# Rows of attention projected before they are weighed, the last rows added in halves, and filler products left out

## The reference

```python
x = x + tanh(g_xattn[0]) * attention(norm(x), ctx, wq, wk, wv, wo)   # keys and values: context rows, then own rows
x = x + tanh(g_ffn[0])   * swiglu_ternary(norm(x), w1, w3, w2)       # weights rounded to -1, 0, 1 times their mean size
x = x + tanh(g_xattn[1]) * wkv(decay, bonus, norm(x), ctx)           # a recurrence over the 64 rows of a sequence
x = x + tanh(g_ffn[1])   * experts(norm(x), router, shared, experts) # 2 of 8 experts for each row, and a shared one
```

```python
out  = softmax(q @ concat(ctx, k).T / 16) @ concat(ctx, v)
return out @ wo.T
```

## Time and profile before

| | |
|---|---|
| time, median of 3 runs | 769.02 us (768.88 to 769.07) |
| the profiled execution | 771.49 us |
| its span, first to last instruction | 769.6 us |
| TensorE busy | 725.0 us, 94% |
| VectorE, ScalarE, GpSimd busy | 520.2, 352.4, 330.5 us |
| mean granted clock of TensorE | 0.99 of full speed |

### The profile page before, as it was taken

One profiled execution on the slowest core, in us unless ns is written; L12 is line 12 of the kernel. 1 busy time (PEld: TensorE's weight loads), 2 busy tenths in 40 slices (PEclk: granted clock), 3 DMA queues, 4 the chain that ended last, 5 costly groups with the idle time before them and its releaser, 6 DMA issues. The chain is left out here.

```text
span 769.6 us, 13097 instructions
## 1 busy us (share of the span) xinstructions
PE 725.0 (94%) x4624; PEld 621.1 (81%) x4624; DVE 520.2 (68%) x926; ACT 352.4 (46%) x676; POOL 330.5 (43%) x345
## 2 busy tenths in 40 slices
PE   6998998999999999999999999999999999897996
PEld 6886787788878988788877988788877988686785
DVE  2778586747877387756877478746877477698532
ACT  3556525642465435643465435553365434523231
POOL 2004204543537155443538155453537245275354
PEclk8999999999999999999999999999999999999999
DMA  9142020200122003111032002110022010011111
GB/s 266 52 138 82 1 56 1 68 30 28 49 76 58 28 29 83 55 41 27 21 85 72 27 27 82 55 41 27 14 82 83 19 35 27 29 42 41 56 63 47
DMA packets 36211, 41.24 MB, mean 54 GB/s; under 512 B 3198, under 2 KB 27476, under 8 KB 36180
## 3 DMA queue, kind: packets, MB, share of 16 engines
q1 hardware_dynamic: 36180, 40.83, 17.8%
HBM read 36.49 MB, written 4.33 MB: 53 GB/s over the span
## 5 line engine op out<-in xcount | busy, mean ns | idle before, releaser
L1136 POOL TENSOR_TENSOR hid_l<-act_sb,hid_h 128x512 fp32r<-128x512 f32 x120 | 163.3, 1361 | 205.9 <-ACT hid_h L938 205.6
L1384 DVE SCALAR_TENSOR_TENSOR act_sb<-act_sb,gate_ps 128x512 f32<-128x512 f32 (+1 forms) x128 | 86.7, 678 | 113.0 <-ACT act_sb L920 112.9
L1145 POOL TENSOR_TENSOR act_sb<-act_sb,late 128x512 f32<-128x512 f32 x64 | 93.6, 1462 | 74.1 <-DVE act_sb L1386 71.5
L938 ACT ACTIVATE hid_h<-act_sb 128x512 fp32r<-128x512 f32 (+1 forms) x128 | 80.3, 627 | 95.6 <-POOL act_sb L1145 62.6
L482 PE MATMUL sums<-down_h,hid_h 128*128 128x256 f32 x320 | 92.0, 288 | 5.0 <-POOL hid_l L1136 5.0
L482 PE MATMUL sums<-down_h,hid_l 128*128 128x256 f32 x320 | 90.3, 282 | 0.0
L482 PE MATMUL sums<-down_l,hid_h 128*128 128x256 f32 x320 | 90.2, 282 | 0.0
L920 ACT ACTIVATE act_sb<-gate_ps 128x512 f32<-128x512 f32 x80 | 47.3, 591 | 85.6 <-PE up_ps L482 82.7
L1386 DVE TENSOR_TENSOR act_sb<-act_sb,up_ps 128x512 f32<-128x512 f32 x120 | 82.5, 687 | 4.1
L482 PE MATMUL gate_ps<-zm_h,gate_h 128*128 128x512 f32 x140 | 61.1, 437 | 7.9 <-DVE act_sb L1386 7.9
L482 PEld LDWEIGHTS sums<-down_h,hid_h 128*128 128x128 f32 x320 | 60.7, 190 | 9.4 <-issue 6.9
(11 more groups left out here) (197 smaller groups left out, 1675.5 us busy)
## 6 DMA issues: line engine op xcount, KB each, us to landing
late<-combine_rows SPq DMA_DIRECT2D x64, 256.0 KB, 3.1
ctx_tok<-in_ctx SPq DMA_DIRECT2D x8, 512.0 KB, 4.8
vals<-in_ctx SPq DMA_DIRECT2D x16, 256.0 KB, 5.4
out_x<-late SPq DMA_DIRECT2D x8, 512.0 KB, 3.1
xa<-in_x SPq DMA_DIRECT2D x7, 512.0 KB, 3.5
wk<-in_L_ffn_w SPq DMA_DIRECT2D x2, 682.0 KB
late<-in_L_ffn_w_down SPq DMA_DIRECT2D x1, 1024.0 KB, 6.1
wk<-in_L_ffn_w_gate SPq DMA_DIRECT2D x2, 512.0 KB, 4.6
```

The lines of the kernel that those rows point to most:

```text
L938: nc.scalar.activation(hid_h[0:n, pos], act_sb[0:n, pos], ACT.Copy).then_inc(hid_h_set, 1)
L1136: nc.gpsimd.tensor_tensor(hid_l[:, pos], act_sb[:, pos], hid_h[:, pos].bitcast(F32), ALU.subtract).then_inc(hid_l_set, 1)
L1145: nc.gpsimd.tensor_tensor(act_sb[:, pos], act_sb[:, pos], comb_sb[:, pos], ALU.mult).then_inc(weighted, 1)
L1384: nc.vector.scalar_tensor_tensor(mine, mine, 1.0, gate_ps[pos][0:hidden_rows(chunk)], ALU.add, ALU.mult).then_inc(gated_one, 1)
```

## The change

Since (p @ v) @ wo.T equals p @ (v @ wo.T), the projection by `wo` is moved ahead of the weighing by the softmax. The own values come out projected at once, because `wv` and `wo` are multiplied once at the start (`turn_wv`, `fuse_wv_wo`). The context rows are projected in every turn by a new step `context_out`, which multiplies the keys' copy of them by `wo` in 16 products of 256 columns, each into 64 rows of a bank; four copies of ScalarE put them into `vals`. `attend` then takes the turned probabilities as the stationary side, 64 rows by 256 columns, and its result is already wo0 and wo1. `project`, the copies of oT0 and oT1, and the two transfers into `vals` are gone. `wo` is loaded ahead of the context rows.

VectorE's order in the full turns: the second value scan and two divisions go ahead of `row_max`, and chunk 6's gate goes behind `add_attention` and `statistics`. GpSimd's `row_factors` and ScalarE's `normalise` for z1T are each moved ahead by a step.

The fillers of the second turn (52 products) go, and in the first turn four groups (6, 3, 30 and 6 products around `q_and_k`, `attend` and z1T; the one ahead of z0T goes from 10 to 4).

In the closing turn each `m_down` comes one chunk later. In the last turn the sums are added and sent out in two halves, the first as soon as the first bank's products are done.

```diff
 TRANSIT = [
-    ... ("A", "v0"), ("A", "v1"), ("A", "scores"), ("A", "pT"),
-    ("A", "oT0"), ("A", "oT1"), ("A", "wo0"), ("A", "wo1"), ...
+    ... ("A", "v0"), ("A", "v1"), ("A", "u0"), ("A", "u1"),
+    ("A", "scores"), ("A", "pT"), ("A", "wo0"), ("A", "wo1"), ...
...
# SyncE
             def attention_weights():
...
+                sp.dma_start(wo[:], woT.rearrange("(k p) e -> p k e", p=P)).then_inc(wo_in, 16)
             def other_weights():
...
-                sp.dma_start(wo[:], woT.rearrange("(k p) e -> p k e", p=P)).then_inc(wo_in, 16)
...
-                    sp.dma_start(vals[S:P, :, 0], ctx_seqs[t.i, 0]).then_inc(ctx_val_in, 16)
-                    sp.dma_start(vals[0:S, :, 1], ctx_seqs[t.i, 1]).then_inc(ctx_val_in, 16)
...
+                    if t.last:
+                        for pair in range(2):
+                            two = slice(2 * pair, 2 * pair + 2)
+                            sp.wait_ge(rows_half, pair + 1)
+                            sp.dma_start(out_rows[t.i - LAG["M"]][:, two], out_row[:, two]).then_inc(out_done, 16)
...
# TensorE
+            def turn_wv():
+                pe.wait_ge(qkv_in[2], 16)
+                for m in range(KH):
+                    for k in range(KH):
+                        last = nc.tensor.transpose(gate_ps[0][:, m * D + k * P:m * D + (k + 1) * P], raw_wv[:, k, m * P:(m + 1) * P], ident[:])
+                last.then_inc(fuse_turned, 1)
+            def fuse_wv_wo():
+                pe.wait_ge(fuse_kept, 1)
+                pe.wait_ge(wo_in, 16)
+                for k in range(KH):
+                    for m in range(KH):
+                        last = nc.tensor.matmul(up_ps[0][:, k * D:(k + 1) * D], wv_turned[:, m, k * P:(k + 1) * P], wo[:, m],
+                                                start=m == 0, stop=m == KH - 1)
+                last.then_inc(fuse_done, 1)
+            def context_out(t):
+                wait_taken(pe, t, "A", "ctxT0", "ctxT1", claims=("A", "u0"))
+                for pair in range(2):
+                    bank, full = claim(t, "A", f"u{pair}")
+                    for r in range(2):
+                        for k in range(KH):
+                            for q in range(2):
+                                last = nc.tensor.matmul(bank[(1 - q) * S:(2 - q) * S, r * D:(r + 1) * D], keys[:, k, 2 * pair + r, 1 + q],
+                                                        wo[:, k], start=k == 0, stop=k == KH - 1)
+                    last.then_inc(full, 1)
             def attend(t):
-                wait_taken(pe, t, "A", "v0", "v1", "pT", claims=("A", "oT0"))
-                pe.wait_ge(ctx_val_in, t.count("A", 32, 32))
-                for h in range(KH):
-                    bank, full = claim(t, "A", f"oT{h}")
-                    for r in range(NT):
-                        for q in range(2):
-                            cols = slice((2 * r + q) * S, (2 * r + q + 1) * S)
-                            last = nc.tensor.matmul(bank[:, cols], vals[:, r, q, h * P:(h + 1) * P], probsT[:, cols],
-                                                    start=True, stop=True)
-                    last.then_inc(full, 1)
-            def project(t):
...
+                wait_taken(pe, t, "A", "v0", "v1", "u0", "u1", "pT", claims=("A", "wo0"))
                 for pair in range(2):
                     bank, full = claim(t, "A", f"wo{pair}")
                     for r in range(2):
-                        for k in range(KH):
-                            last = nc.tensor.matmul(bank[:, r * D:(r + 1) * D], qo[:, k, (2 * pair + r) * P:(2 * pair + r + 1) * P],
-                                                    wo[:, k], start=k == 0, stop=k == KH - 1)
+                        for q in range(2):
+                            tile = 2 * pair + r
+                            cols = slice((2 * tile + q) * S, (2 * tile + q + 1) * S)
+                            last = nc.tensor.matmul(bank[q * S:(q + 1) * S, r * D:(r + 1) * D], probsT[:, cols], vals[:, tile, q],
+                                                    start=True, stop=True)
                     last.then_inc(full, 1)
...
             def turn(t):                                    # full turns and turn 0
                 if first:
                     keep_clock(12)
+                    turn_wv()
                 context_T(t)
...
                 if first:
-                    keep_clock(10)
+                    fuse_wv_wo()
+                    keep_clock(4)
                 z_T(t, "A", "z0T", za_row, 1)
                 m_up(4)
                 m_down(2)
-                if first:
-                    keep_clock(6)
                 q_and_k(t)
                 values(t)
+                context_out(t)
                 m_down(3)
                 scores(t)
...
                 attend(t)
                 m_up(6)
-                if first:
-                    keep_clock(3)
-                project(t)
                 m_up(7)
                 m_down(5)
                 m_up(8)
                 m_down(6)
-                if first:
-                    keep_clock(30)
                 z_T(t, "A", "z1T", za_row, 2)
...
-                if first:
-                    keep_clock(6)
                 f_up(0)
...
             def second(t):
                 q_and_k(t)
                 values(t)
                 keys_T(t)
+                context_out(t)
                 scores(t)
-                keep_clock(10)
                 probs_T(t)
-                keep_clock(3)
                 attend(t)
-                keep_clock(3)
-                project(t)
-                keep_clock(30)
                 z_T(t, "A", "z1T", za_row, 2)
-                keep_clock(6)
                 f_up(0)
...
             def closing(t):
                 m_up(2)
-                m_down(0)
                 keys_T(t)
                 for c in range(3, MC - 1):
                     m_up(c)
-                    m_down(c - 2)
+                    m_down(c - 3)
                 y_T(t)
                 m_up(MC - 1)
+                m_down(MC - 4)
                 m_down(MC - 3)
...
# ScalarE
+            def context_out(t):
+                for pair in range(2):
+                    bank = wait_full(act, t, "A", f"u{pair}")
+                    for q in range(2):
+                        half = slice((1 - q) * S, (2 - q) * S)
+                        last = nc.scalar.activation(vals[half, 2 * pair:2 * pair + 2, q],
+                                                    bank[half].rearrange("p (r d) -> p r d", r=2), ACT.Copy)
+                    last.then_inc(free_of("A", f"u{pair}"), 1)
...
                 normalise(t, "A", 1, xa, za_row, rstd_a, shift_a)
+                if first:
+                    high("wv")
...
                 values(t)
+                context_out(t)
...
                 probs_T(t)
-                attend(t)
...
                 m_chunk(6)
+                normalise(t, "A", 2, xa, za_row, rstd_a, shift_a)
                 m_chunk(7)
-                normalise(t, "A", 2, xa, za_row, rstd_a, shift_a)
...
# GpSimd
+                row_factors(t, "A", 2, mv_a, nmean_a, var_a, rstd_a, shift_a)
                 m_weigh(6)
                 m_low(6)
-                row_factors(t, "A", 2, mv_a, nmean_a, var_a, rstd_a, shift_a)
...
# VectorE
                     add_to_values(t, 0)
+                    scan_values(t, 1)
+                    divide(t, 0, 0)
+                    divide(t, 0, 1)
                 row_max(t)
                 m_gate(5)
                 row_scale(t)
...
                 if w:
-                    scan_values(t, 1)
-                    divide(t, 0, 0)
-                m_gate(6)
-                if w:
-                    divide(t, 0, 1)
                     quotient(t, 0)
                 add_attention(t)
                 wait_taken(dve, t, "A", "wo0", "wo1")
                 statistics(t, "A", 2, xa, bn_a, mv_a)
+                m_gate(6)
...
             def last(t):
-                add_sums(t, "M", gain_m[:, 0:1], experts_in(t)[0], out_row)
+                dve.wait_ge(out_done, t.count("M", 16, 0))
+                for pair in range(2):
+                    two = slice(2 * pair, 2 * pair + 2)
+                    if pair:
+                        dve.wait_ge(down_done, chunk_no(t, ("M", MC - 1)))
+                    else:
+                        dve.wait_ge(sums_half, 1)
+                    nc.vector.scalar_tensor_tensor(out_row[:, two].rearrange("p r d -> p (r d)"), sums[pair][:], gain_m[:, 0:1],
+                                                   experts_in(t)[0][:, two].rearrange("p r d -> p (r d)"), ALU.mult, ALU.add).then_inc(rows_half, 1)
```

(25 more changed lines are left out.)

15 lines of the change are left out of this document (6 added, 9 removed), and 4 rows, old and new, of the table TRANSIT.

## The result

The kernel after takes 758.68 us (median of four runs, 757.72 to 759.49) against 769.05 for the kernel before beside it: ratio 0.985, interval 0.982 to 0.989. A second series gave 758.44 against 771.01, ratio 0.984 (0.981 to 0.987). The profiled execution takes 759.49 us with a span of 757.8, 11.8 shorter than before's.

A forecast was written before the change was run, and what follows sets the result against it. PE (TensorE) was taken to bound the six steady turns. -11.0 there, +2.2 + 1.5 first turn, +0.6 + 2.1 second, -0.9 closing, -1.1 last make -6.6 us: 769.02 to 762.4 us, range 757.8 to 768.2 (forecast's own 759.6 to 766.6).

The forecast's parts named there:

- c: Steady turns: time per instruction of `context_out` and the new `attend` on PE, 0.110 us (0.102 to 0.122).
- an allowance: Steady turns: 0.11 us per turn taken off the gain for changes between full and half width (nothing to 0.3).
- the z1T wait: Steady turns: PE's wait for ScalarE's normalised rows, 0.46 us per turn, was expected to go.
- the first rival: Steady turns: array halves do not run side by side, PE pays more; 778.9 or 795.5 us; chance 0.08.
- rule of weight loads: PE: a load runs beside a product only if row groups differ; here no load would hide, giving 778.9 us.
- the second rival: Steady turns: another engine takes the freed time, making `m_down(6)` wait; 768.4 to 773.4 us; chance 0.14.
- the sum for the load of `wo` and the fillers: First turn: load of `wo` 1.0 us, filler and weight products 0.9 us more; z0T 1.2 us late.
- What the prediction called covered: Second turn: VectorE's idle 2.25 + 0.78 us before `add_attention` covers 3.0 of `row_max`'s 3.6 us delay, leaving +0.6.
- The price of the low clock: First two turns: PE's clock falls between `attend` and z1T without fillers, costing +1.5 and +2.1 us.
- The clock does not matter: First two turns: rival that VectorE bounds both anyway, so 758.8 us; chance 0.08.
- The shift: Closing turn: each `m_down` one chunk later lets `keys_T` and VectorE start earlier, -0.9 us (0 to -1.5).
- The halves are 1.4: End of last turn: adding and sending the sums by halves, -1.1 us (0.7 certain, up to 1.4).

The follow-up runs named there:

- e12: Kernel after with every product of `context_out` written to the lower half of its bank, so the output is not the reference's; 785.19 us, single run.
- c_after: Kernel after, unchanged, measured again as the second series; 758.44 us (757.69 to 759.5), ratio 0.984 to the kernel before.
- e3: Kernel after with the two 256 KB loads into `vals` issued again in every turn, only as a burden; 760.43 us (759.08 to 762.2).
- e1: Kernel after with the removed fillers put back at their old places in the first two turns; 756.89 us (754.54 to 759.54).
- e7: Kernel after with fillers put back, longer ahead of z1T (42 and 46) and f_up(0) (8), plus 8 each side of z3T; 755.31 us (753.92 to 756.77).
- e9: Kernel after with `context_out` behind `scores`, its second pair first, in the first two turns only; 752.7 us (751.64 to 754.09), ratio 0.976 to before.
- e4: Kernel after with the closing turn in its old order, m_down(0) ahead of `keys_T` and each `m_down` one chunk earlier; 760.92 us (759.21 to 763.19).
- e11: Kernel after with the last rows added and stored whole, as in the kernel before; 759.82 us in the one run.
- e8: Kernel after with both `context_out` behind `scores` in every turn and the longer fillers (46 in the second turn); 758.35 us (756.45 to 758.84).
- e6: Kernel after with `context_out` moved behind `scores`, and behind the softmax on ScalarE, in every turn; 757.82 us (756.96 to 759.64).
- first four experiments: e1, fillers taken out of the kernel before (780.3 us), e3 and e4.
- e5: Kernel after with loops of `context_out` and `attend` turned, so 4 and 2 products of one array half come in a row; 766.05 us, single run.
- e13: Kernel after with `context_out`'s loops turned so that two products of one array half come in a row; 760.71 us, single run.
- e10: e9 with fillers sized by the waits in the first two turns and 8 each side of z3T; 748.7 us (746.96 to 751.9), ratio 0.971 to before.

## Why the prediction was right and where it was wrong

**Steady turns: right.** c was 0.113 and 0.118 us against 0.110 and an allowance, the z1T wait went: -10.5 for -11.0. What made this wait go, the shorter `attend` or the steps that the change moved on VectorE, GpSimd and ScalarE, was not tested apart. The halves do work side by side (e12), so the first rival is out by its own price: c is under the 0.129 from which it decides, and in one half the steady turn would be 3.45 us longer. The Trainium skill (TensorE: Matmul & The Clock Gate, Part 3, Measured speedup vs the span model) gives 2.38 times for three products packed by columns; two by turns give 1.94 here (7.12/3.67). The Trainium skill's rule of weight loads (the same page, The mechanism), which the prediction set against the change, is not borne out here: by it the prediction had 0.157 us for an instruction, which would have left no gain, and the trace has 0.113; the measurement decides. Of the second rival nothing came: no wait for `hid_l`.

**First turn: wrong, and this is the step that failed.** "I take z0T 1.2 us late (0.2 to 2.7)": it came 3.1 us early, and the turn took 0.9 us more (0.2 less in c_after) in place of 3.7 more. The prediction asked of the two loads into `vals` only whether PE waits for a transfer in the steady turns, and put them at nothing. In the first turn they were under way with the context rows, the transfer that PE waits for longest there. e3 puts them back, and the rows, the clock and z0T are late again, z0T by 1.5 us against before: the sum for the load of `wo` and the fillers was sound, the loads were the missing term. The Abs of after is then 1.95 us late, not 4.8. Against that, the low clock cost 2.2 to 3.7 us there (e1, e7), not 1.5. Of this, 1.15 is its fall under the first queries, where 6 fillers had gone, which one of the two profiles of after has; the other 2.2 to 2.6 lie behind z1T.

**Second turn: right in sum.** +2.2 for +2.7; the clock costs 1.4 of it (e7) where 2.1 was said, which leaves 0.8 for the order where 0.6 was. What the prediction called covered could have been a gain: e9 takes 3.4 us from this turn by the place of `context_out` alone.

**The price of the low clock: right in sum.** 3.6 us was said for both turns; e7, which keeps the clock up in both, gains 4.0 there in its profile and 3.1 in the median. The same fillers as before give back only 1.5 to 1.8 (e1). "The clock does not matter" is out.

**Closing and last: mis-sized.** The shift is 1.7 us (e4), said 0.9; the wait for y_T's products was missed. The halves are 1.4 (e11), the upper bound, where 1.1 was taken. Another 1.5 of the profiles' difference is the fall of the clock in before's execution. The three come to 4.6 us where the profiles differ by 4.4; the 0.2 too much can't be assigned.

**Sum.** With what was measured for the mis-sized steps (first turn +0.9 for +3.7, second +2.2, steady -10.5, closing -1.7, last -1.4) the change is -10.5 us; the medians of the first series differ by 10.4. Of the some 3.8 us by which the gain is larger than forecast, the first turn makes 2.8, the closing turn 0.8, the second 0.5 and the last 0.3, and the steady turns take 0.5 back. That the sum closes to 0.1 is partly luck: its terms come from single profiles, and what stays open is how much each execution owes to the clock (the first turn of after is 76.87 and 75.72 in two of them).

## What to carry to other kernels

A transfer that no engine is seen waiting for can still delay the one that is waited for: look at what shares the queues with it in the start-up, not only at the waits in the steady loop. What a filler of the clock is worth depends on the work behind it on the chain: shorten that first (10 us became 3 or less), and then size each filler by its wait, since too long can be as dear as none (e8 against e6). Judge an edit by stages; e6's total hid a gain of 5 us and a loss of 4.

## What the runs showed of the hardware

The kernel before takes 766.7 to 774.1 us from run to run, in step with the granted clock: among the runs of the first four experiments the shortest span, 764.8, has a mean of 0.996, the longest, 771.4, one of 0.988. Behind one and the same wait, 1.9 us at the head of the closing turn, the clock fell within 2 us in 5 of the 16 profiled executions (before, e6, e7, e9 and e12) and not in the others; why in these is open. In the kernels that differ from after only ahead of that turn, z3T comes 49.9 to 50.2 us behind the cut where it fell (e6, e9, e12) and 48.7 to 48.9 where it did not (after, c_after, e1, e3, e5, e13): 1.0 to 1.5 us. In e6, e9 and e12 it did not fall again behind z3T (granted 1.00 from 48 to 65 us behind the cut), as it did in c_after (0.90), and their closing and last turn are only 0.3 to 0.7 us longer than c_after's. e10, which bridges most waits of the first two turns and z3T, has spans of 744.7 and 745.8 with clock 1.00 and one of 750.1 with 0.993.
